# Moving work around the seam between a delta-rule phase and a tile loop: gate weights loaded and unpacked earlier, another split of the last solve, one copy issued sooner

## What is computed

```python
x = _layernorm(x + _L0_attn_ref(x, ...))     # gated delta rule, 8 heads of 128, two keys per token
x = _layernorm(x + _L0_xattn_ref(x, ...))    # cross attention, 16 heads, a mask of 9 keys by seg_id
x = _layernorm(x + _L0_ffn_ref(x, ...))      # silu(x Wg) * (x Wu), then Wd

def _dequant(wq, scale):                      # the FFN's weights come as int32
    return (wq.astype(jnp.float32) - ZERO_POINT) * scale[:, None]
```

## Time and profile before

| | |
|---|---|
| median of 3 runs | 1204.29 us (1203.63 to 1205.12) |
| the profiled execution | 1203.97 us |
| its span, first to last instruction | 1202.2 us |
| busy: PE, PEld | 1125.5 us (94%), 780.2 us (65%) |
| busy: DVE, ACT, POOL | 823.7 us (69%), 702.5 us (58%), 518.4 us (43%) |
| chain that ended last | PE 74%, DVE 9%, POOL 7%, ACT 3%, issue 3%, SP's queue 2%, DMA 1% |

### The profile page before, as it was taken

One profiled execution on the slowest core, in us unless ns is written; L12 is line 12 of the kernel. 1 busy time (PEld: TensorE's weight loads), 2 busy tenths in 40 slices (PEclk: granted clock), 3 DMA queues, 4 the chain that ended last, 5 costly groups with the idle time before them and its releaser, 6 DMA issues.

```text
span 1202.2 us, 28714 instructions
## 1 busy us (share of the span) xinstructions
PE 1125.5 (94%) x11460; PEld 780.2 (65%) x11460; DVE 823.7 (69%) x1447; ACT 702.5 (58%) x1212; POOL 518.4 (43%) x717
## 2 busy tenths in 40 slices
PE   7788899999999999999989799859999999999997
PEld 2444455555555555655555566649899989989976
DVE  5887768878778779778776455675655666565552
ACT  3776567676776767777668566524444444444443
POOL 1659485684783974964867511330110000010000
PEclk9999899999999999999999799969999999999999
DMA  4123235545454554656546312431122221112100
GB/s 120 45 54 80 68 51 79 115 79 87 98 80 84 107 90 79 117 117 135 101 81 219 90 41 72 167 110 45 45 50 52 52 66 49 45 45 51 30 14 9
DMA packets 147268, 93.74 MB, mean 78 GB/s; under 512 B 80672, under 2 KB 130720, under 8 KB 146240
## 3 DMA queue, kind: packets, MB, share of 16 engines
q1 hardware_dynamic: 145984, 91.71, 34.7%
q10 hardware_dynamic: 1152, 0.21, 0.1%
HBM read 54.77 MB, written 14.55 MB: 58 GB/s over the span
## 4 chain that ended last, share of the span: by engine, by line
PE 74%; DVE 9%; POOL 7%; ACT 3%; issue 3%; SPq 2%; DMA 1%; ACTq 0%; DVEq 0%; POOLq 0%
PE proj L499 21%; PE out L1594 5%; PE turned_v_chain L1594 5%; PE gram L514 4%; PE proj L1653 4%; PE turned_v_chain L1663 4%; PE proj L1533 3%; DVE conv L1081 3%; POOL inverse L1296 2%; POOL rank_one L1293 2%; PE gram L1568 2%; PE out L523 2%; PE turned_v_chain L505 2%; PE decays L530 2%; PE turned_v_chain L645 1%
## 5 line engine op out<-in xcount | busy, mean ns | idle before, releaser
L1081 DVE SCALAR_TENSOR_TENSOR conv<-proj,kq_weights,conv 128x504 f32<-128x504 f32 (+2 forms) x261 | 189.8, 732 | 32.5 <-ACT conv L811 26.2
L499 PE MATMUL proj<-xT,vg_weights 128*128 128x512 f32 x384 | 191.2, 621 | 3.0 <-DVE conv L1081 1.9
L1891 POOL TENSOR_TENSOR rope<-rope_part,rope_part 128x512 f32<-128x512 f32 x32 | 40.0, 1271 | 320.6 <-DVE rope_part L1833 320.6
L1081 DVE SCALAR_TENSOR_TENSOR conv<-proj,vg_weights,conv 128x504 f32<-128x504 f32 (+2 forms) x192 | 140.7, 733 | 45.7 <-ACT conv L811 40.7
L499 PE MATMUL proj<-xT,kq_weights 128*128 128x512 f32 x348 | 166.9, 606 | 0.2 <-DVE conv L1081 0.2
L1296 POOL TENSOR_TENSOR inverse<-inverse,rank_one 128x30 f32<-128x30 f32 (+14 forms) x240 | 124.9, 521 | 18.8
L1293 POOL TENSOR_TENSOR rank_one<-inverse 128x30 f32<-128x30 f32 (+14 forms) x240 | 118.7, 495 | 15.0
L499 PEld LDWEIGHTS proj<-xT,vg_weights 128*128 128x128 f32 x384 | 68.9, 194 | 67.2 <-issue 61.0
L499 PEld LDWEIGHTS proj<-xT,kq_weights 128*128 128x128 f32 x348 | 62.4, 190 | 74.3 <-issue 70.3
L1672 ACT ACTIVATE rstd<-rstd 128x1 f32<-128x1 f32 x48 | 9.7, 202 | 144.7 <-DVE rstd L1780 144.7
L514 PEld LDWEIGHTS gram<-keys_q 128*64 128x64 f32 x896 | 57.6, 138 | 53.9 <-ACT keys_q L822 36.4
(11 more groups left out here) (256 smaller groups left out, 2503.1 us busy)
## 6 DMA issues: line engine op xcount, KB each, us to landing
kq_weights<-in_kq_w SPq DMA_DIRECT2D x32, 390.0 KB, 6.6
vg_weights<-in_vg_w SPq DMA_DIRECT2D x32, 390.0 KB, 6.2
o_scratch<-oT SPq DMA_DIRECT2D x32, 256.0 KB, 2.2
o_in<-o_scratch SPq DMA_DIRECT2D x16, 512.0 KB, 4.0
o_rs<-o_rs_quarters SPq DMA_DIRECT2D x88, 64.0 KB, 6.0
diagonal<-gram_decayed SPq DMA_DIRECT2D x128, 32.0 KB
inverse<-inverse SPq DMA_DIRECT2D x32, 128.0 KB, 2.9
q_first<-rope SPq DMA_DIRECT2D x128, 32.0 KB, 1.9
```

The lines of the kernel that those rows point to most:

```text
L499: mm = e.matmul(bank(c, u)[:], w[:, (k * 3 + c % 3) * 128:(k * 3 + c % 3 + 1) * 128], xT[g][:, k, :], start=(k == 0), stop=(k == KD - 1))
L1081: e.scalar_tensor_tensor(acc(c, u)[:, :, back:], src[:, :, 0:S - back], weights(c, u)[:, j:j + 1], acc(c, u)[:, :, back:], ALU.mult, ALU.a ...
L1891: e.tensor_tensor(turned[half][:].rearrange("p b r q -> p r b q"), parts[2 * half][:], parts[2 * half + 1][:], op).then_inc(s_turned, 1)
```

## The change

1. **Gate weights.** The tiles that are dead early (`between_lhs`, `between_rhs`, `causal`, `w_ab`, `decay`, `beta_turned` and five of the ten tiles `q_sq`) now lie together in a region `gate_weights`. In slot 37 SP loads gate's ints there and all three scales (up's go into the region `prepare`), behind five waits, the first for the o sums of unit 26. In slot 39 DVE unpacks gate. What is left in slot 41 is `w_uvo` and the ints of up and down, and `unpack_down` and the unpacking of up wait for those (32) and for the four early loads (64).
2. **The last batch's shares.** `LAST_CUTS` takes the place of `CUTS` for batch 7.
3. **One inverse copy.** In slot 32 the high half of batch 6's inverse is issued ahead of the store of o and of the diagonal copies of unit 31, not behind them.

```diff
+    def skip(self, region):
+        self.regions[region][0] = self.at
...
 CUTS = (((1, 1), (1, 1), (1, 5)), ((5, 10), (10, 13), (13, 16)), ((16, 19), (19, 22), (22, 25)), ((25, 31), (31, 31), (31, 31)))
+LAST_CUTS = (((1, 1), (5, 13), (1, 5)), ((13, 13), (13, 21), (21, 21)), ((21, 21), (21, 31), (31, 31)), ((31, 31), (31, 31), (31, 31)))
...
+                def gate_weights():
+                    e.wait_ge(s_osum, U - NS - 1)
+                    e.wait_ge(s_between, U)
+                    e.wait_ge(s_steps, U)
+                    e.wait_ge(s_eem, U)
+                    e.wait_ge(s_solve, SOLVE * (NB_SOLVE - 1) + READY)
+                    e.dma_start(ints["w_gate"][:].rearrange("p k n -> p (k n)"), a["gate_w"]).then_inc(d_gate, 16)
+                    for n in ("gate", "down", "up"):
+                        e.dma_start(scales[f"w_{n}"][:], a[f"{n}_scale"]).then_inc(d_gate, 16)
...
+                    if s == U:
+                        store_inverse_high(solve_at(s, 8))
...
-                    if h is not None and s > LAG:
+                    if h is not None and s > LAG and s != U:
                         store_inverse_high(h)
...
+                    if s == last_slot - 3:
+                        gate_weights()
...
+                    if s == last_slot - 1:
+                        ahead["dequantize"]("w_gate")
...
+                    cuts = (LAST_CUTS if h == NB_SOLVE - 1 else CUTS)[cut]
...
                 def dequantize(n):
-                    e.wait_ge(done["ints"], 96)
+                    e.wait_ge(done["scales"], 64)
+                    if n == "w_up":
+                        e.wait_ge(done["ints"], 32)
...
                         if s == AHEAD:
-                            dequantize("w_gate")
                             dequantize("w_up")
```

More of the change, by code:

```diff
@@ L176, in delta_phase @@
         room.open("rest")
+        ones_mean = t("ones_mean", [128, 128])
+        onorm = t("o_norm_w", [128, 1])
+        guard = t("guard", [128, 1])
+        even, odd = t("even", [128, 1]), t("odd", [128, 1])
+        dt = t("dt_bias", [128, H])
+        rate = t("rate", [128, H])
+        q_sq = {i: t(f"q_sq{i}", [128, GB, S]) for i in (7, 8, 9, 0, 1)}
+        room.open("gate_weights")
+        q_sq.update({i: t(f"q_sq{i}", [128, GB, S]) for i in range(2, 7)})
         between_l = t("between_lhs", [128, T])
@@ L207, in delta_phase @@
         ints = {}
[L208 to L210 removed]
+        for n, shape, region in (("w_gate", [128, KD, FI], "gate_weights"), ("w_up", [128, KD, FI], "chain"),
+                                 ("w_down", [128, FJ, D], "chain")):
+            ints[n] = room.again(region, f"{n}_ints", shape, I32, keep=True)
+            tiles[n] = room.again(region, f"t_{n}", shape)
         tiles["w_uvo"] = room.again("chain", "t_w_uvo", [128, XH // 2, D])
@@ L394, in weights_after_chain @@
                     e.dma_start(tiles["w_uvo"][:], scratch["w_uvo"]).then_inc(d_uvo, 16)
-                    for n, k in (("w_gate", "gate"), ("w_up", "up"), ("w_down", "down")):
+                    for n, k in (("w_up", "up"), ("w_down", "down")):
                         e.dma_start(ints[n][:].rearrange("p k n -> p (k n)"), a[f"{k}_w"]).then_inc(d_ints, 16)
-                        e.dma_start(scales[n][:], a[f"{k}_scale"]).then_inc(d_ints, 16)
+                def gate_weights():
[7 more added lines that the diff above has]
+                        e.dma_start(scales[f"w_{n}"][:], a[f"{n}_scale"]).then_inc(d_gate, 16)
                 e.dma_start(w_ab[:], a["w_ab"]).then_inc(d_wab, 16)
@@ L1417, in delta_phase @@
     tiles["ints"], tiles["scales"] = ints, scales
-    done = {"o": s_og, "w_high": s_whiout, "scaled": s_gr, "stored": d_out, "weights": d_w, "first": d_first, "uvo": d_uvo, "ffn": s_wgt, "ints": d_ints, "decays": s_ee,
+    done = {"o": s_og, "w_high": s_whiout, "scaled": s_gr, "stored": d_out, "weights": d_w, "first": d_first, "uvo": d_uvo, "ffn": s_wgt, "ints": d_ints, "scales": d_gate, "decays": s_ee,
             "gram": s_gm, "gate": s_silu[G], "v1": s_conv[V1], "high": s_wlo, "low": s_wloout, "solve": s_solve}
```

23 lines of the change are left out of this document (10 added, 13 removed).

## The result

The changed kernel takes 1191.33 us (median of 4 runs, 1187.83 to 1192.44) beside 1203.96 for the kernel before on the same chip (4 runs); the ratio is 0.9887, interval 0.9862 to 0.9913, or 10.5 to 16.6 us less. Two more sets of six runs on other chips gave 0.9885 (0.9859 to 0.9912) and 0.9913 (0.9892 to 0.9933). The profiled execution took 1192.44 us (span 1190.6) beside 1203.97 (1202.2). The forecast was 1192.2.

A forecast was written before the change was run, and what follows sets the result against it. It took TensorE to bound the tile loop, so its earlier idle time counts one for one: 4.2 (shares) + 7.6 (gate weights) = 11.8 us off 1203.97 gives 1192.2 us, range 1188.0 to 1196.4.

The forecast's parts named there:

- Part 1: Last solve's shares: steps 10 to 12 fill POOL's gap, `W_scaled` of unit 26 comes sooner; gain 4.2 us (3.6 to 4.6).
- the gap: POOL's idle time ahead of `W_scaled` of unit 24, forecast to fall from 4.63 us to under 0.5.
- the forecast spans: PE's waits in slots 35 and 36: from 1.82 and 4.07 us to under 1 and to 2 to 3.
- Part 2: Gate weights loaded and unpacked early: PE goes on at 800.1, not 807.67, in the loop's first slot; gain 7.6 us (5.5 to 10.5).
- The softmax's product: DVE, loop's first slot: ready at 786.61, it waits for POOL's first unpacking instruction until 787.7 and ends at 788.9.
- DVE in slot 39: Unpacking gate there takes about 2.3 us, mostly covered by 2.14 us of idle time; cost 0, upper bound 0.5.
- SP in slot 37: Four more issues, 2.6 us, go ahead of weights needed a slot later; cost 0.
- The clash of DVE and POOL: Loop's first slot: a DVE instruction waits for POOL's running one; gain 7.6 us with this rule, 10.5 without.
- Part 3: High copy first: PE's 2.96 us wait in slot 33 moves ahead of the projection of g; gain 0, clock cost up to 1.0.
- The rival of the late diagonals: High copies overlap the diagonal copies by 1.7 us and delay POOL's scaling as much: 1193.9 us; chance 0.03.
- The unpacking of gate: A sign: DVE unpacks gate near 734, taking 2.3 to 3.4 us.
- The clock: PE's slow stretch behind slot 36's wait (0.50, 680 to 685) stays, effect 0; rival that it stays up, 1188, chance 0.12.

The follow-up runs named there:

- shares_alone: The kernel before with only the last solve's new shares (`LAST_CUTS`): 1198.38 us, ratio 0.9953.
- after_again: The changed kernel run again unchanged, for more times and a second profile: median 1189.83 us (6 runs).
- high_alone: The kernel before with only the high inverse copy issued ahead of the store and the diagonals: 1203.99 us, ratio 1.0006.
- after: The first profile of the changed kernel, nothing else edited: profiled execution 1192.44 us, median of its runs 1191.33 us.
- after_third: The changed kernel run once more unchanged, on another chip: 1190.43 us (6 runs), ratio 0.9913.
- gate_late: The changed kernel with gate unpacked again in the tile loop's first slot, ahead of up, but still loaded in slot 37: 1195.04 us, ratio 0.9934.
- down_pieces: The changed kernel with POOL's two instructions that unpack down cut into eight each: 1193.57 us, ratio 0.9915.
- down_vector: The changed kernel with down loaded ahead of up and unpacked on DVE, not POOL, ahead of the softmax's sum: 1186.40 us, ratio 0.9862.
- gate_alone: The kernel before with only the gate weights' early load (slot 37) and unpacking (slot 39): 1194.99 us, ratio 0.9927.

## Why the prediction was right, step by step

- **Part 1**, 4.2 us (3.6 to 4.6): the gap went to 0.48, as forecast (under 0.5), and `W_scaled` of unit 26 came 4.04 us sooner after the scaling; 4.3 in shares_alone. The difference to the 4.63 of the working is in single steps of POOL that took longer, each with a DVE instruction beside it: `W_scaled` of unit 25 took 1.57 us in this profile and 1.04 in others. That DVE is the cause is my reading; no run separates it. By whole runs it is 5.7 us (3.7 to 7.5), so the size is borne out but not sharply; in shares_alone's profile another 1.5 us come behind `W26`, ahead of the cross projection (102.84 in place of 104.37), which the working had left out. PE's waits of 0.53 and 2.84 lie in the forecast spans (under 1, 2 to 3).
- **Part 2**, 7.6 us (5.5 to 10.5): 8.36 in the profile; by runs 8.8 (5.7 to 11.8). Compared at one length of the cross projection, kernels without and with the part differ by 24.90 - 15.02 = 9.9 us (6.6 to 6.7 us, before and after_again), 22.45 - 16.54 = 5.9 (5.1, high_alone and after) and 23.32 - 15.78 = 7.5 (3.69, shares_alone and after_third) from the cross projection to `turn_x1`. All lie between the forecast bounds; that the first profile came within 0.8 of 7.6 is partly luck. Single steps of the working came out otherwise. Down landed 12.5 us after its issue, and POOL began at 782.80; measured from the cross projection that is 1.4 us later than forecast (0.97 after it, and not 782.3 - 782.77 = -0.5). The softmax's product did not wait for POOL's first instruction: it ran beside it in 1.84 us, 0.6 over its 1.22, and in after_third it was not slowed at all (rows below). And POOL's second instruction took 4.53 and not 5.54. The first makes it worse and the other two better, and the layernorm ended at 792.93, 11.1 us after the cross projection began; forecast was 794.6 - 782.8 = 11.8. Behind `turn_x1` the forecast kept everything as it was; to rope 3 it took 9.28 us in place of 10.01, 0.7 less. The product of after_third, on DVE, and POOL's instruction, inside which it lies:

```profile
783.34 1.22 DVE L1853 TENSOR_TENSOR att<-att,total 128x1024 f32<-128x1024 f32 x1
```

```profile
779.72 5.37 POOL L1925 TENSOR_SCALAR t_w_down<-w_down_ints 128x2048 f32<-128x2048 int32 x1 [1.73 <-DMA w_down_ints<-in_down_w]
```

- DVE in slot 39 and SP in slot 37 at nothing: right. The copy of Y starts 0.16 us later than the 0.93 by which this slot is shifted; gate_late, which frees the place, gains nothing there.
- The clash of DVE and POOL, which separated 7.6 from 10.5: shown by down_pieces (0.42 for the layernorm) and by down_vector, where POOL is gone and so is the wait. The sum had two waits in it, 1.1 us of the softmax's product for POOL's first instruction and 2.9 of the layernorm for the second. The second is there (3.71 us in place of 0.41), the first is not. The Trainium skill (GPSIMD Engine Reference, Key points) names contention on the shared SBUF interfaces, for VectorE instructions in a 2-port mode or with two SBUF inputs. The traces agree that the two engines clash here, but the softmax's product, with two such inputs, lost 0.6 us or nothing, and the layernorm's, with one, stood until POOL was done. Whether that one ran in a 2-port mode no run here shows.
- **Part 3** at nothing: right, by the forecast's own reason, since PE's wait moved to DVE's convolution: 5.11 us with late diagonals, 3.90 and 3.88 with timely ones (after_again, after_third), where "about the same length" as 2.96 was forecast. The rival of the late diagonals seemed to have come true in the profile, with 1.18 us. The repeated profiles refute it as a fixed delay: they are late or on time in either order. A delay that is only more frequent is not excluded.
- The unpacking of gate ran at 737.13 and not near 734: up to there the part 1 gain was mostly offset by the +1.85 and +1.18.
- **The clock** behind slot 36 stayed at 0.50 from 680 to 685, as assumed. The profile's total agreed with the forecast to 0.2 us partly by luck: the two parts and the clock behind them gave 4.04 + 9.09 = 13.1 us and not 11.8, and +1.85, +1.18, +0.07 and -1.6 elsewhere, which no part was forecast to bring, took 1.5 back.

## What to carry to other kernels

A wait can cost TensorE twice: its own length, and the lower clock behind it. How much comes on top is not told by the length. Ahead of `turn_x1` it was, by what the way to rope 3 took beyond 7.7 us, 1.6 us behind 3.47 and behind 2.57, 2.8 behind 2.99, 2.7 behind 3.14, nothing behind 2.03, 0.70 and 0.17; and the wait of 1.9 us ahead of the last tiles cost 1.6 us in seven profiles and nothing in seven. So remove the last wait of a chain wholly, where that is cheap: shortening it to 2.57 gave no gain that the runs could tell, and cutting POOL's work into pieces cost 3.7 us. Where a VectorE instruction takes several times its usual duration and ends together with a GpSimd one, try taking the work off GpSimd before reordering the two: DVE had 5 us of idle time for what cost GpSimd 10.9 us.

And before a microsecond in one profile is given to a change, take the unchanged program's profile again: here it explained a shift that one pair of experiments had seemed to confirm.

## What the runs showed of the hardware

- GpSimd and DVE get in each other's way, but not all instructions alike. `TENSOR_SCALAR` of 128x256, 0.41 us alone, took 3.71 and ended 0.15 us behind GpSimd's `TENSOR_TENSOR`; before the change it took 4.42 and ended 0.15 us behind GpSimd's `TENSOR_SCALAR`. A `TENSOR_TENSOR` of 128x1024, 1.22 us alone, took 1.84 (after) and 2.10 (gate_alone) in the middle of GpSimd's `TENSOR_SCALAR`, and 1.22 there in after_third; what makes the difference is open.
- A GpSimd instruction cut into eight cost 7.27 us in place of 5.37 and 7.69 in place of 4.53 to 5.54, with DVE working beside it.
- Unpacking 2048 integer columns: 10.9 us on GpSimd in two instructions, 2.35 to 2.56 on DVE in one pass.
- The same program's executions differ in single places: in three profiles of the changed kernel the diagonals came after 9.8 or 11.1 us, and the cross projection took 3.69, 5.09 or 6.74 us behind the same wait of 2.7 us. Across kernels, with the same instructions and the same wait of 1.9 us, the last part took 68.4 or 70.0 us. The 6 to 7 us between the fastest and the slowest run of the changed kernel on one chip are of the size of such steps together; that they are made of them is an estimate.
